# Query made transposed from its weights, weight splits moved beside the FFN, query blocks in rising order, W in the output bank

## The reference

```
xn = layernorm(x)                                  # no affine part
q = xn @ Wq.T        -> 32 heads of 128, rotated:  q*cos + rotate_half(q)*sin
k = rope part (32+32 of each 128) from xn @ Wkr.T, rotated; the rest from (xn @ Wdk.T) @ Wupk.T
v = (xn @ Wdk.T) @ Wupv.T                          # 8 key/value heads, each shared by 4 query heads
attn = softmax(causal(q k^T / sqrt(128)))          # 1024 x 1024
ffn = (silu(xn @ W_gate.T) * (xn @ W_up.T)) @ W_down.T      # 1792 hidden
out = x + (attn v) @ Wo.T + ffn
```

## Time and profile before

| | us |
|---|---|
| three timed runs, median (lowest to highest) | 2536.4 (2534.0 to 2538.39) |
| the profiled execution, its own time | 2536.75 |
| its span | 2534.2 |
| PE busy | 2425.0 (96%) |
| DVE busy | 1538.5 (61%) |
| ACT busy | 1180.4 (47%) |
| POOL busy | 798.9 (32%) |
| mean granted clock of TensorE | 0.989 of full |

### The profile page before, as it was taken

How to read it: one execution, slowest core, us unless ns; L and a number is a source line. 1 busy time by engine, 2 the same in 40 slices (tenths; PEclk the granted TensorE clock), 3 DMA queues, 4 the chain that set the end, 5 groups by cost and what they waited for, 6 DMA issues and landing times.

```text
span 2534.2 us, 41298 instructions
## 1 busy us (share of the span) xinstructions
PE 2425.0 (96%) x12352; PEld 2008.1 (79%) x12352; DVE 1538.5 (61%) x3993; ACT 1180.4 (47%) x2317; POOL 798.9 (32%) x815
## 2 busy tenths in 40 slices
PE   6999999996899999999999999999999999999999
PEld 5777778775788888878888888788888888888887
DVE  4333232322667677767676776677677767776775
ACT  2433424242444555545454554445455545545544
POOL 1000000000434444434343443434434434344442
PEclk9999999997999999999999999999999999999999
DMA  6536173444211101010101121211101010101000
GB/s 198 161 112 168 56 198 106 124 143 181 96 34 34 39 31 51 34 51 18 51 18 51 34 101 55 81 34 34 51 18 51 34 51 18 51 18 51 1 10 25
DMA packets 93871, 169.22 MB, mean 67 GB/s; under 512 B 6368, under 2 KB 56032, under 8 KB 87904
## 3 DMA queue, kind: packets, MB, share of 16 engines
q1 hardware_dynamic: 91552, 162.55, 20.3%
q10 hardware_dynamic: 2112, 4.19, 0.5%
HBM read 116.39 MB, written 50.33 MB: 66 GB/s over the span
## 4 chain that ended last, share of the span: by engine, by line
PE 71%; issue 3%; DVE 1%; ACT 0%; POOL 0%; DMA 0%; DVEq 0%; SPq 0%; ACTq 0%; POOLq 0%
PE ob L1037 15%; PE scores L1016 15%; PE misc L996 14%; PE misc L1048 14%; PE ptb L1026 10%; PE misc L1003 2%; DVE wo L971 0%; DVE qT L940 0%; DMA wq_raw<-in_wq 0%; DVE oT L949 0%; POOL prob L854 0%; ACT wo L906 0%; DVE nmax L923 0%; DVE q_cos L934 0%; DVE prob L923 0%
## 5 line engine op out<-in xcount | busy, mean ns | idle before, releaser
L854 POOL TENSOR_TENSOR prob<-prob,rinv 128x512 f32<-128x512 f32 (+7 forms) x512 | 579.6, 1148 | 677.0 <-DVE rinv L963 675.5
L882 ACT ACTIVATE prob<-prob,nmax 128x512 f32<-128x512 f32 (+7 forms) x512 | 397.2, 776 | 370.8 <-DVE nmax L923 360.4
L891 ACT ACTIVATE pT<-ptb 128x512 fp32r<-128x512 f32 x576 | 335.3, 594 | 424.1 <-PE ptb L1026 412.6
L1037 PE MATMUL ob<-pT,v_sb 128*128 128x512 f32 x1728 | 515.5, 416 | 0.0
L1016 PE MATMUL scores<-kT,qT 128*128 128x512 f32 (+3 forms) x2304 | 481.9, 349 | 1.2 <-DVE nmax L923 0.7
L945 DVE TENSOR_TENSOR pT<-ptb,pT 128x512 fp32r<-128x512 f32 x576 | 393.5, 686 | 100.8 <-ACT pT L891 94.5
L1016 PEld LDWEIGHTS scores<-kT,qT 128*128 128x128 f32 x2304 | 380.5, 189 | 55.6 <-issue 2.7
L923 DVE CUSTOM_DVE_ANT_0 prob<-scores,mask 128x512 f32<-128x512 f32 (+7 forms) x512 | 381.0, 752 | 38.2 <-issue 35.8
L996 PE MATMUL misc<-wq,xT 128*128 128x512 f32 x1536 | 384.3, 400 | 18.7 <-DVE wq L967 17.1
L1048 PE MATMUL misc<-wo,oT 128*128 128x512 f32 x1536 | 375.3, 393 | 27.6 <-issue 15.0
L996 PEld LDWEIGHTS misc<-wq,xT 128*128 128x128 f32 x1536 | 287.9, 191 | 84.1 <-issue 20.9
(11 more groups left out here) (74 smaller groups left out, 2115.5 us busy)
## 6 DMA issues: line engine op xcount, KB each, us to landing
ff_raw<-in_ffw SPq DMA_DIRECT2D x56, 384.0 KB, 3.0
k_parts<-stage SPq DMA_DIRECT2D x128, 128.0 KB, 2.4
v_parts<-stage SPq DMA_DIRECT2D x64, 256.0 KB, 3.5
wq_raw<-in_wq SPq DMA_DIRECT2D x16, 1024.0 KB, 5.0
kT<-k_parts SPq DMA_DIRECT2D x16, 1024.0 KB, 6.5
v_sb<-v_parts SPq DMA_DIRECT2D x16, 1024.0 KB, 6.5
wo_raw<-in_wo SPq DMA_DIRECT2D x16, 1024.0 KB, 5.0
xT_parts<-xT SPq DMA_DIRECT2D x16, 512.0 KB, 7.2
```

Of the source, the lines that this page charges most:

```text
L854: nc.gpsimd.tensor_tensor(prob[:, n % 2, h, 0:W], prob[:, n % 2, h, 0:W], rinv[:, hd % 8:hd % 8 + 1].broadcast_to([P, W]), ALU.mult)\
L882: nc.scalar.activation(prob[:, n % 2, j, 0:W], prob[:, n % 2, j, 0:W], ACT.Exp, bias=nmax[:, hd % 8:hd % 8 + 1], scale=-1.0, accum_out=rsu ...
L891: nc.scalar.activation(pT[:, t % 4, HI], ptb[t % 2][:], ACT.Copy).then_inc(pT_hi, 1)
L1037: mm = nc.tensor.matmul(ob[:], v_sb[:, e % 2, x, j], pT[:, t % 4, y], start=(j == 0 and (x, y) == (HI, HI)), stop=(j == i and x == LO))
```

## The change

Four parts.

1. **q.** The weights of one query head are the stationary side and 512 tokens of xT the moving one, so that q comes out transposed, in its own bank `qb`: one Q operation makes one head for four blocks (`AHEAD` = 4 blocks; Q of unit n is head n % 4 of tokens half n // 4 % 2). DVE rotates it in that layout (three operations over 512 columns, two of them on 64 partitions), POOL adds once, ACT and DVE split from `q_cos` in SBUF (QL). QT is gone. `qT` holds two halves of four heads.
2. **Weights.** Wq and Wo are split in stage 1, once: eight FFN steps of every chunk fetch 512 KB, split it (`keep_hi` on ACT, `keep_lo` on DVE, 1024 columns) in the buffers `w_raw2` and `stage`, and store 1 MB to DRAM (`keep_w`). Stage 2 loads the split parts: `wq` in four pieces per head, `wo_a` double, `wo_b` single. XQ and XO are gone. To make room, `prob` of heads 2 and 3 and `oT` are single and `pT` has three buffers.
3. **Order.** Blocks come in rising order 0 to 7. `product_order` is new (below), `STEP` is gone.
4. **W** goes into `ob`, as PV does. PV of a unit waits for the addition of W of the unit before.

xT goes to DRAM and back in one DMA of 2 MB per chunk. SP's loads are written out without loops.

```diff
 def product_order(units):
-    (the walk over STEP)
+    out = [("Q", m, 0) for m in range(AHEAD)]
     for k in range(units + 2):
         if k % UNITS == EARLY and k < units:
             out.append(("CUT", k - EARLY, 0))
+        blocks = key_blocks(k - 1) if 1 <= k <= units else 0
+        s = [("S", k, j) for j in range(GRP)] if k < units else []
+        q = [("Q", k + AHEAD, 0)] if k + AHEAD < units else []
+        t = [("T", k - 1, j) for j in range(blocks)]
+        pv = [("PV", k - 1, j) for j in range(blocks)]
+        out += s[:2]
+        if k >= 2:
+            out.append(("W", k - 2, 0))
+        for j in range(blocks):
+            out += t[j:j + 1] + (pv[j - LAG:j - LAG + 1] if j >= LAG else [])
+        left = pv[max(blocks - LAG, 0):]
+        if blocks > LAG:
+            out += s[2:3] + left[:1] + s[3:] + left[1:] + q
+        elif blocks == LAG:
+            out += s[2:] + left + q
+        else:
+            out += s[2:] + q + left
     return out
...
+            def fetch_w(c, c1, u):
+                sp.wait_ge(w_kept_lo, c1 * SPLIT_BLOCKS + u - 1)
+                sp.dma_start(w_raw2[:, u % 2 * 2:u % 2 * 2 + 2], a["wqo"][c * SPLIT_BLOCKS + u])\
+                    .then_inc(w_fetched[u % 2], 16)
+            def keep_w(c, c1, u):
+                sp.wait_ge(w_kept_lo, c1 * SPLIT_BLOCKS + u + 1)
+                sp.dma_start(scr["w"][c * SPLIT_BLOCKS + u].rearrange("p h x d -> p (h x d)"),
...
                 sp.dma_start(ff_out[:], a["x"][c]).then_inc(res_loaded, 16)
-                with sp.Fori(1, MB // 2) as m2:
-                    for o in range(2):
-                        load_ff(c1, m2 * 2 + o, o)
+                for u in range(2):
+                    fetch_w(c, c1, u)
+                for m in range(2, MB):
+                    load_ff(c1, m, m % 2)
+                    if 3 <= m < 3 + SPLIT_BLOCKS:
+                        keep_w(c, c1, m - 3)
+                    if 3 <= m < 1 + SPLIT_BLOCKS:
+                        fetch_w(c, c1, m - 1)
...
+            def keep_hi(c1, u2, p):
+                nc.scalar.activation(stage[:, 2 * p:2 * p + 2, HI], w_raw2[:, 2 * p:2 * p + 2], ACT.Copy)\
+                    .then_inc(w_kept_hi, 1)
...
+            def keep_lo(c1, m, p):
+                nc.vector.tensor_tensor(stage[:, 2 * p:2 * p + 2, LO], w_raw2[:, 2 * p:2 * p + 2],
+                                        stage[:, 2 * p:2 * p + 2, HI].bitcast(F32), ALU.subtract)\
...
+                if ge:
+                    sp.wait_ge(wo_b_used, ge)
+                sp.dma_start(wo_b[:]...)
...
                     elif kind == "Q":
-                        (four operations over 256 columns)
+                        nc.vector.tensor_tensor(q_sin[0:HALF], qb[HALF:P], sin[HALF:P], ALU.mult)
+                        nc.vector.tensor_tensor(q_sin[HALF:P], qb[0:HALF], sin[0:HALF], ALU.mult)
+                        nc.vector.tensor_tensor(q_cos[:], qb[:], cos, ALU.mult).then_inc(q_read, 1)
+                    elif kind == "QL":
+                        nc.vector.tensor_tensor(q[:, LO], q_cos[:], q[:, HI].bitcast(F32), ALU.subtract)\
...
                         for k in range(KC):
-                                mm = nc.tensor.matmul(misc[:], xT[:, i, x, k], wq[:, w, k],
+                                mm = nc.tensor.matmul(qb[:], wq[:, h, w, k], xT[:, x, p, k],
...
                         if j == 0:
-                            pe.wait_ge(o_split, it1 * UNITS + n)
+                            pe.wait_ge(acc_done, it1 * UNITS + n)
...
-                                mm = nc.tensor.matmul(misc[:], oT[:, u, x, h * P:(h + 1) * P], wo[:, w, h],
+                        heads = (2, 3, 0, 1) if i == TB - 1 else (0, 1, 2, 3)
+                                mm = nc.tensor.matmul(ob[:], oT[:, x, h * P:(h + 1) * P], w[:, y],
```

More of the change, by code:

```diff
@@ L68 @@
 EARLY = 2
+AHEAD = 4
+SPLIT_BLOCKS = 8
 def unit_kv(n):
     return n // TB
-ORDER = [TB - 1 - j // 2 if j % 2 else j // 2 for j in range(TB)]
 def unit_block(n):
-    return ORDER[n % TB]
+    return n % TB
 def key_blocks(n):
@@ L92, with query_of @@
 KEYB = first_key_block(UNITS)
+def query_of(n, j):
+    return n // AHEAD * AHEAD + j
 def product_order(units):
[L101 to L102 removed]
+    out = [("Q", m, 0) for m in range(AHEAD)]
     for k in range(units + 2):
@@ L151, in followers @@
     if kind == "S":
[L152 to L166, removed]
+        return [("dve", "S", n, j, 1.35 * cols + 0.1), ("act", "EXP", n, j, 1.1 * cols + 0.35),
+                ("dve", "INV", n, j, 0.16), ("pool", "NORM", n, j, 2.0 * cols + 0.1)]
+    if kind == "Q":
+        return [("dve", "Q", n, j, 2.0), ("pool", "Q", n, j, 1.1),
+                ("act", "QL", n, j, 0.6), ("dve", "QL", n, j, 0.85)]
+    if kind == "W":
+        return [("dve", "W", n, j, 0.7)]
+    if kind == "T" or is_last(kind, n, j):
+        return [("act", kind, n, j, 0.6), ("dve", kind, n, j, 0.7)]
+    return []
 def orders():
-    cost = {"Q": 2.6, "QT": 0.44, "T": 0.44, "PV": 0.65, "W": 2.6}
+    cost = {"Q": 2.72, "T": 0.44, "PV": 0.7, "W": 2.72}
     free = dict(act=0.0, dve=0.0, pool=0.0)
@@ L212, in orders @@
             waits.append(("dve", "T", n, j))
+            if j == 0 and n:
+                waits.append(("dve", "W", n - 1, 0))
         while ready and (ready[0][0] <= now or any(w not in done for w in waits)):
@@ L216, in orders @@
             now = max(now, done[w] + 0.05)
-        now += 3 * key_blocks(n) * P * 0.00042 + 0.1 if kind == "S" else cost[kind]
-        for gap, chain in followers(kind, n, j):
+        now += 3 * key_blocks(n) * P * 0.00044 + 0.1 if kind == "S" else cost[kind]
+        chain = followers(kind, n, j)
+        if chain:
             serial += 1
@@ L221, in orders @@
                 early.update(step[:4] for step in chain)
-            ready.append((now + gap + 0.05, serial, chain))
+            ready.append((now + 0.05, serial, chain))
             ready.sort()
@@ L311, in key_value_and_ffn @@
         xT_stored = sem("xT_stored")
+        w_fetched = [sem(f"w_fetched{i}") for i in range(2)]
+        w_kept_hi = sem("w_kept_hi")
+        w_kept_lo = sem("w_kept_lo")
+        w_kept = [sem(f"w_kept{i}") for i in range(2)]
         ff_loaded = [sem(f"ff_loaded{i}") for i in range(2)]
@@ L496, in chunk @@
                     nc.scalar.activation(dst, ring[n % RING][:], ACT.Copy).then_inc(hi_ready, 1)
-                with act.Fori(0, MB // 2 - 1) as m2:
+                with act.Fori(0, SPLIT_BLOCKS // 2) as m2:
+                    for o in range(2):
+                        gate(c1, m2 * 2 + o, o)
+                        cast_gate_up(c1, m2 * 2 + (o + 2), o)
+                        cast_down(c1, m2 * 2 + (o + 1), 1 - o)
+                        keep_hi(c1, m2, o)
+                with act.Fori(SPLIT_BLOCKS // 2, MB // 2 - 1) as m2:
                     for o in range(2):
@@ L836, in _ @@
+            for i in range(TB):
+                store_out(B - 1, i)
             sp.wait_ge(stored, 16 * B * TB)
```

411 lines of the change are left out of this document (201 added, 210 removed).

## The result

The changed kernel takes 2663.2 us (median of four runs, 2655.9 to 2665.2) against 2535.6 for the kernel before on the same chip: 1.050 times as long, 95% interval 1.0475 to 1.0519. It is slower by 128 us; 2635 was forecast, with a range of 2562 to 2695. The profiled span is 2663.4 us against 2534.2, so 129.2 us have to be found.

The account below looks back on a forecast made before the run. The prediction took TensorE, busy for 96% of the span, as the bound; +5.0 us a round over sixteen rounds gave +80, the FFN +18, so 2536.75 + 80 + 18 = 2635 us, range 2562 to 2695.

Parts of the forecast that it names:

- The wait at the third transposition: Attention: T2 waits for T0's split in six of eight units, 1.45 us each, 8.7 us a round.
- W of block 0: Attention: block 0's W waits for o's copy and split behind two short S, 1.3 us a round.
- rival (c): TensorE's clock: short waits bring it to 1.2 GHz for a tenth of the stage, about 2820 us; chance 0.03.
- Rival (b): Transposition chain in attention: under 1.63 us the change wins, 2502 us; chance 0.11.
- the FFN's +18: FFN stage: 12 us from weight fetches ahead of ff_raw's third load, 6 from later steps' DMA traffic.
- QT's 0.40: TensorE in attention: q's four transpositions, removed, save 0.40 us per block, 3.2 us a round.
- The chain of 2.10 us: Attention: from T0's start through ScalarE's copy and VectorE's subtraction until TensorE runs again, 2.10 us.
- least stall: Third transposition: T0 and T1 fill 0.80 of the 2.10 us, so at least 1.30 us is waited.
- a PV, S or W always stood in between: Attention's old order: T0, T1 and T2 were always separated by another product; no size of its own.
- 0.3 (unit of two blocks): Attention: PV0 comes 1.9 us after T0's start against 2.10 needed, 0.3 us a round.
- 0.5 (QL from SBUF): VectorE in attention: q's split subtraction with two SBUF inputs instead of one in PSUM, 0.5 us a round.
- tail and start together 0, give or take 6: Attention stage's start and end: changed loads and the largest unit last together cost 0, give or take 6 us.

Follow-up runs that it names:

- Experiment 5: Changed kernel with each unit's first transposition put ahead of W (both, for units of two key blocks): 2609.2 us, 1.0278 of the kernel before.
- experiment 9: Changed kernel with W and S woven between first transpositions, cut after step 6, FFN's third load before weight fetches: 2524.4 us, 0.9949 of the kernel before.
- experiment 7: Kernel before with q's four transpositions of each unit issued twice: 2582.5 us, 1.0175 of the kernel before.
- experiment 4: Changed kernel with ff_raw's third load issued ahead of a chunk's first two weight fetches: 2651.3 us, 1.0456 of the kernel before.
- experiment 2: Changed kernel with the loop cut after step 6 instead of step 2: 2652.3 us, 1.046 of the kernel before.

## Why the prediction was right

**Right.** The wait at the third transposition: 96 times, 1.45 us each, as in the term 8.7 a round, with the releaser named. W of block 0: 20.6 us in 18 places, the 1.3 a round that I took. The clock stayed at 1.00 in the steady rounds, against rival (c). Rival (b), a chain under 1.63 us, fell: T2 starts 2.0 to 2.7 us behind T0 in every unit. (It was priced with 5.6 us saved where the prediction's own terms give 5.8, and without the FFN's +18.) Experiment 5 bears the cause out, by taking the wait away and 54 us with it, and experiment 9, by 7.4 us a round.

**Terms that were mis-sized.** QT's 0.40 is 0.347 (experiment 7), so -2.8 and not -3.2 a round. The chain of 2.10 us is no floor: in the unit of eight blocks T2 starts 2.01 us behind T0 and the wait is 0.98 (1.14 with the tail, under the "least stall" of 1.30), in the other units 1.21 to 1.42 in the records. q's three rotations take 0.69, 0.68 and 0.69 us, 2.1 and not 1.9. And that "a PV, S or W always stood in between" before is too strong: 64 pairs of transpositions stand directly behind one another there (one is the x8 of the earlier trace rows), but never three. The terms 0.3 (unit of two blocks) and 0.5 (QL from SBUF) don't show as waits; QL's mean is 0.792, under the 1.026 that I had as the upper bound, and what it adds is inside the ptb wait, as the 0.81 above. A round without a jump is +3.9, where the sum said +5.0; with the measured terms -2.8 - 2.6 + 8.7 + 1.3 = +4.6, and 0.7 are unplaced.

**The step that failed in attention** is "tail and start together 0, give or take 6": the start is +9.3. The first Q stands 9.6 us behind the stage's start instead of 7.6, and three of the first Q wait 7.0 us for the rotation of the one before them, with a mean granted clock of 0.72 from 641.6 to 665 us.

**The step that was missing** is the jump: six pauses of 4.8 us and what TensorE then runs at the lower level, 37 us. The change kept the cut after step 2, but what was in flight there, and what the engines did first behind it, changed. I had read the clock and the waits of one steady window that holds no jump.

**FFN** was +18 and is +23.4. The queue's order was the right cause: ring waits for ff_w 13.0 us and not 2.3, 10.7 more, and experiment 4 gives 12 back. What was left out is the clock behind the wait:

```profile
253.78 5.53 PE L657 MATMUL ring<-xT,ff_w 128*128 128x512 f32 x16 [2.75 <-ACT ff_w L454]
...
260.97 3.79 PE L657 MATMUL ring<-xT,ff_w 128*128 128x512 f32 x16
```

The sixteen products behind the wait take 5.53 us instead of 3.91, since the granted clock was 0.60 from 253.8 to 256.0 (1.00 in the same place before). In the four chunks they take 6.51, 5.53, 5.37 and 3.93 us, 5.8 more than before together; hidden products wait 4.4 more (6.8 against 2.4). 10.7 + 5.8 + 4.4 = 21, and 2.5 are not placed.

So the sum of 98 missed 129 by 31: rounds 18 too high (1.1 x 16), jumps 37, start and end 7, FFN 5 too low. The total came out within the range partly by luck: the rounds were put too high while the jumps, which alone are worth more than a quarter of the loss, stood nowhere in the sum.

## What to carry to other kernels

When work is taken from a pipelined order, look at what it covered: here the step and the wait removed were worth 5.4 us a round, and the cover lost between the first three transpositions cost 8.7. A cover moved to close one wait opens the one it closed before (Q's), so list for each long product what waits behind it, and choose one that is nobody's. In a loop, read one window that holds the jump, look at what each engine still has to do when it jumps, and keep large loads and the critical chain away from it; and price every wait of several us with the slower clock that follows it.

## What the runs showed of the hardware

- At a loop's jump a 16 KB packet of the instruction queue started 2.5 to 2.6 us before TensorE's first product in 24 of 24 pauses. The pause was 3.8 to 5.3 us in the changed kernel and with the cut after step 10 (DMA share 0.69 to 0.98 during it), 2.7 on average with the loads held back; in the kernel before, twelve products covered it. Which engine is late depends on the place (ScalarE 2.4 us in experiment 2, with a DMA share of 0.02).
- In the changed kernel the mean granted clock was 0.50 to 0.64 over the 2.7 us behind each idle time of 2.9 us and more (eight of them), and six score products took up to 2.28 us instead of 1.23. Behind 91 waits of 1.0 to 1.8 us it stayed at 1.00. In between both occurred: 0.60 behind 2.26 us, 1.00 behind 2.15.
- VectorE's subtraction over 512 columns with both inputs in SBUF (QL) took 0.686 us on average where no GpSimd operation ran beside it (65 of 128) and 0.901 where one did (63, at most 1.32), against 0.687 with one input in PSUM.
